# Sixty units become thirty-three in the first layer of a graph kernel, and all eight blocks take single rows

## The reference

```
dst   = sort(int(12500 * u**2))                 # 200000 edges, u uniform in 0..1
msgs  = layernorm(x)[src] * edge_weight
x1    = x + segment_sum(msgs, dst) @ W.T + b
```

```
h      = layernorm(x1) @ W_gat                  # 16 values a node: 4 heads x 4 experts
e      = leaky_relu(a_src[src] + a_dst[dst])
alpha  = segment_softmax(e, dst)
scores = layernorm(segment_sum(h[src] * alpha, dst) + b_gat), mean over heads
top 2 of the 4 scores are the gates
out    = x1 + sum_e gate_e * (gelu(y @ W1[e] + b1[e]) @ W2[e] + b2[e])   # y = layernorm(x1)
```

## Time and profile before

| | us |
|---|---|
| median of 3 runs | 3705.21 (3705.07 to 3710.14) |
| the profiled execution | 3709.83 |
| its span in the profile | 3708.0 |
| PE busy | 3033.7 (82%) |
| POOL busy | 2700.9 (73%) |
| DVE busy | 2035.0 (55%) |
| ACT busy | 819.2 (22%) |

### The profile page before, as it was taken

The page is one execution under the profiler, slowest core; times in us unless marked ns, Lnnn a source line. Parts: engine busy times, 40 slices in busy tenths (PEclk is TensorE's granted clock), DMA queues, the critical chain, the costliest instruction groups (busy, mean ns, idle before and its releaser), DMA issues. The chain is left out here.

```text
span 3708.0 us, 65908 instructions
## 1 busy us (share of the span) xinstructions
PE 3033.7 (82%) x13893; PEld 2476.2 (67%) x13894; DVE 2035.0 (55%) x6854; ACT 819.2 (22%) x2321; POOL 2700.9 (73%) x2803
## 2 busy tenths in 40 slices
PE   1666667667777777887899799999999999999748
PEld 1454445555565555665677588888888888888637
DVE  8875566576667767666664322353434343343567
ACT  6300000100111111111122222222332223222247
POOL 6677777777777777777677477777777777777573
PEclk6788887887888878788899899999999999999979
DMA  9633333434444444444344122232322222223279
GB/s 346 209 115 105 108 108 110 115 113 114 117 118 114 118 118 120 118 124 118 106 125 133 51 72 54 53 112 63 75 57 73 54 72 60 73 54 75 65 281 381
DMA packets 280932, 426.20 MB, mean 115 GB/s; under 512 B 63672, under 2 KB 214499, under 8 KB 279651
## 3 DMA queue, kind: packets, MB, share of 16 engines
q0 software_dynamic: 113760, 216.95, 23.2%
q1 hardware_dynamic: 68911, 114.88, 8.5%
q10 hardware_dynamic: 98004, 91.50, 7.6%
HBM read 317.12 MB, written 105.98 MB: 114 GB/s over the span
## 5 line engine op out<-in xcount | busy, mean ns | idle before, releaser
L712 POOL DMA_INDIRECT rows<-feats,src_t x1500 | 1459.6, 973 | 484.0 <-issue 453.5
L881 PE MATMUL node_sums<-rows,ys_ahead 128*128 x3904 | 1063.5, 432 | 479.7 <-DVE ys_ahead L942 244.8
L881 PEld LDWEIGHTS node_sums<-rows,ys_ahead 128*128 128x128 f32 x3904 | 817.0, 216 | 683.9 <-issue 550.2
L1286 POOL DMA_INDIRECT got<-row_dram,src_sorted x1010 | 977.2, 968 | 308.1 <-issue 308.1
L1369 PE MATMUL d_hidden<-d_yt,w 128*128 128x256 f32 x3136 | 711.2, 380 | 0.8 <-DVE d_yt L1455 0.8
L1380 PE MATMUL d_expert<-w,hid 128*128 128x256 f32 x3136 | 708.7, 379 | 0.0
L1380 PEld LDWEIGHTS d_expert<-w,hid 128*128 128x128 f32 x3136 | 595.8, 190 | 81.0
L1369 PEld LDWEIGHTS d_hidden<-d_yt,w 128*128 128x128 f32 x3136 | 593.7, 191 | 80.3 <-DVE d_yt L1455 1.2
L1432 DVE TENSOR_TENSOR yo<-d_expert,x_and_b 128x512 f32<-128x512 f32 x196 | 135.5, 691 | 839.8 <-PE d_expert L1380 832.2
L942 DVE TENSOR_SCALAR ys_ahead<-iota,rel,ew_t 128x128 f32<-128x128 f32 x1952 | 557.2, 361 | 66.4 <-DVE rel L938 3.8
L1313 ACT ACTIVATE hid<-d_hidden,b1c 128x256 f32<-128x256 f32 x784 | 324.4, 471 | 982.5 <-PE d_hidden L1369 793.4
(11 more groups left out here) (303 smaller groups left out, 2315.0 us busy)
## 6 DMA issues: line engine op xcount, KB each, us to landing
y_dram<-yo ACTq DMA_DIRECT2D x196, 256.0 KB
ys<-y_dram SPq DMA_DIRECT2D x36, 1024.0 KB, 9.2
got<-row_dram SPq DMA_DIRECT2D x1792, 0.1 KB
rows<-feats,src_t POOLq DMA_INDIRECT x1500
got<-row_dram,src_sorted POOLq DMA_INDIRECT x1010, 2.4
ys_ahead<-y_dram SPq DMA_DIRECT2D x13, 1024.0 KB, 9.1
x_dram<-edge_plan ACTq DMA_DIRECT2D x98, 128.0 KB
d_x<-x_dram ACTq DMA_DIRECT2D x49, 256.0 KB
```

The costliest lines, as they stand in the source:

```text
L712: pool.indirect_dma_start(rows[:, g % RING, j, :], None, feats, bass.IndirectOffsetOnAxis(ap=m.src_t[:, g * GT + j:g * GT + j + 1], axis=0 ...
L881: t = pe.matmul(psA[:, ds(((code >> 1) & 1) * 512, FEAT)], hot[:, r, j, :], rows[:, ds((code >> 2) & (RING - 1), 1), j, :], start=False, s ...
L1286: pool.indirect_dma_start(got[:, k, j, 0:ROWF], None, m.row_dram, bass.IndirectOffsetOnAxis(ap=m.src_sorted[:, BEGIN[b] + j:BEGIN[b] + j + ...
```

## The change

The loop is cut into 33 units. Behind each of the first 16, DVE makes four histogram pieces and then one whole sort piece; units 16 to 23 have a sort piece only (unit 16 also the positions), units 24 to 32 have nothing. PE counts the four pieces in the same unit, and makes the transposes at the end of the unit whose sort piece asks for them. In the second stage the last block takes single rows too, and those of block 0 are issued ahead of the wait for the spreads and the load of `adst`. POOL gathers 1008 columns instead of 1010.

```diff
-        PIECES, UNITS = 24, 60
...
+        PIECES, UNITS = 24, 33
+        COUNTED = 16
+        PER = HPIECES // COUNTED
```

PE, behind each unit:

```diff
-                if n >= 1:
-                    for q in hist_at[n - 1]:
-                        count(q)
+                if n < COUNTED:
+                    for q in range(PER):
+                        count(n * PER + q)
                 if n == COUNTED:
                     pe.matmul(psC[:, 0:TILES], zero_b[:, 0:P], zero_b[:, 0:TILES], start=False, stop=True
                               ).then_inc(s_hm, 1)
-                if n == COUNTED + 2:
                     pe.wait_ge(s_cnt, 1)
...
-                if n in TURN_AT:
-                    k = TURN_AT[n]
-                    pe.wait_ge(s_turn, k + 1)
+                if n >= 9 and n < PIECES - 1:
+                    pe.wait_ge(s_turn, n - 8)
                     for q in range(GCOLS // P):
...
-                if n == SORTED + 1:
+                if n == PIECES - 1:
```

DVE, behind each unit:

```diff
-                if n in sort_at:
-                    buf = sort_piece(*sort_at[n], buf)
-                if n == SORTED:
+                if n < COUNTED:
+                    for q in range(PER):
+                        hots(n * PER + q)
+                if n == COUNTED:
+                    positions()
+                if n < PIECES:
+                    buf = sort_piece(n, buf)
+                if n == PIECES - 1:
                     sort_end(buf)
-                if n == SORTED + 2:
-                    segments()
-                for q in hist_at[n]:
-                    hots(q)
-                if n == COUNTED + 1:
-                    counts()
-                if n == COUNTED + 3:
-                    positions()
```

`counts` is now the head of `positions`, and `segments` the tail of `sort_end`. The second stage:

```diff
-        single = lambda b: SINGLE if b < BLOCKS - 1 else 0
-        in_quarter = lambda b, q: max(0, min(size(b) - single(b), (q + 1) * QUARTER) - q * QUARTER)
+        in_quarter = lambda b, q: max(0, min(size(b) - SINGLE, (q + 1) * QUARTER) - q * QUARTER)
...
             ask(0)
+            single_rows(0)
             sp.wait_ge(m.s_sc, 16 * TILES)
             sp.dma_start(adst[:], m.adst_first[0:GEDGES, :].rearrange("(p j) h -> p j h", p=P)).then_inc(s_ad, 16)
-            single_rows(0)
             for b in range(BLOCKS):
-                if b + 1 < BLOCKS - 1:
+                if b + 1 < BLOCKS:
                     ask(b + 1)
                     single_rows(b + 1)
...
-                for j in range(size(b) - single(b)):
+                for j in range(size(b) - SINGLE):
...
-                if single(b):
-                    v.wait_ge(s_single, 16 * (1 + SINGLE * P) * (b + 1))
+                v.wait_ge(s_single, 16 * (1 + SINGLE * P) * (b + 1))
```

More of the change, by code:

```diff
@@ L915, in _ @@
                               ).then_inc(s_hm, 1)
-                if n in TURN_AT:
-                    k = TURN_AT[n]
-                    pe.wait_ge(s_turn, k + 1)
+                if n >= 9 and n < PIECES - 1:
+                    pe.wait_ge(s_turn, n - 8)
                     for q in range(GCOLS // P):
-                        t = pe.transpose(psT[:, q * P:(q + 1) * P], key[turned_keys[k]][:, q * P:(q + 1) * P],
+                        t = pe.transpose(psT[:, q * P:(q + 1) * P], key[turned_keys[n - 9]][:, q * P:(q + 1) * P],
                                          m.ident[:])
                     t.then_inc(s_turned, 1)
-                if n == SORTED + 1:
+                if n == PIECES - 1:
                     pe.wait_ge(s_turn, PIECES - 9)
@@ L989, in exchange, with columns @@
                 return to
-            def columns(buf, n, a, z):
-                for bit in range(bits_of(n) - 1 - a, bits_of(n) - 1 - z, -1):
+            def columns(buf, bits):
+                for bit in range(bits - 1, -1, -1):
                     buf = exchange(buf, bit)
@@ L1001, in take, with sort_piece @@
                 return buf
[L1003 to L1007, removed]
+            def sort_piece(n, buf):
+                if n < 10:
                     flip(buf, n + 1, 0)
[L1009 to L1012, removed]
+                    buf = columns(buf, n + 1)
+                else:
+                    k, back = 11 + (n - 10) // 2, (n - 10) % 2
+                    if back:
+                        buf = columns(take(1 - buf, n - 9), 10)
+                    else:
+                        buf = take(1 if buf != 1 else 0, n - 9)
+                        flip(buf, k, 10)
+                        buf = columns(buf, k - 10)
+                if 9 <= n < PIECES - 1:
                     v.sem_inc(s_turn, 1)
@@ L1037, in sort_end @@
                 c.done(v.tensor_reduce(m.link[:, 1:2], m.seg_keep[:], AX_X, ALU.min))
-            def segments():
                 v.wait_ge(s_turned, PIECES - 9)
@@ L1062, in hots, with positions @@
                 v.sem_inc(s_hh, 1)
-            def counts():
+            def positions():
                 v.wait_ge(s_hm, HPIECES + 1)
@@ L1068, in counts @@
                 v.sem_inc(s_cnt, 1)
-            def positions():
                 v.wait_ge(s_hm, HPIECES + 2)
```

## The result

The changed kernel takes 3644.98 us (3643.43 to 3646.45, 4 runs), the kernel before 3706.56 in the same comparison. The ratio is 0.9832 (0.9815 to 0.9849): 61.6 us faster, where 46 were forecast (3659, range 3638 to 3690). The profiled execution took 3643.7, its span is 3641.8.

A forecast was written before the change was run, and what follows sets the result against it. POOL was taken to bound the first layer to about 1600, PE after that. 17.5 (POOL's waits) + 30 (lag at the end) = 47.5, against it 2 for a lower clock: net -46, 3705.2 to 3659 us, range 3638 to 3690.

The forecast's parts named there:

- POOL keeps 17.5 us: First layer from 1600 on: POOL no longer waits for PE behind a full buffer of gathered groups, 17.5 us won.
- rival (d): First layer: POOL's gathers go faster as DVE's work is bunched, 40 us won, 3619; chance 0.08.
- The lag at the end: End of first layer: PE finishes 10 us behind POOL's last gather instead of 40.3, bounds 6 and 16; 30 us won.
- The colder last stages: End of first layer: PE reaches the four last `stages` with a lower clock than before, 2 us lost.
- The second stage: Its edits (SP's row order, two POOL columns fewer) cost or win 0, bounds -3 to +10; 1386 us as before.
- The units' account: First layer by groups of units, POOL's time against PE's: PE falls 28 behind in units 6 to 15, at most 58.
- the ring: POOL's 16 groups of gathered rows ahead of PE: 82 us, less 4 for a landing; when full, POOL waits.
- B: First layer: fewer interruptions of PE, so fewer cold restarts (steps at the lower clock); 60 units before, 33 after.
- A: First layer: the place of DVE's histogram and sort bursts, none in the last quarter of the units.
- (a): Units 6 to 15: slow return of the clock, or histogram pieces waiting for counts; at x = 5, 3689; chance 0.15.
- (b): Units 6 to 15: clock stays lower for the whole unit after each long idle; 104 net lost, 3809; chance 0.06.
- the signs: Trace marks expected, among them PE waiting in 16 long stretches of 25 to 30 us before 1200, last gather about 2029.

The follow-up runs named there:

- a_per8: The changed kernel with eight histogram pieces a unit in the first 8 units instead of four in 16: 3757.56 us, ratio 1.0142.
- a_no_exchange: The changed kernel without the sort's 306 two-input minima and maxima, so the keys stay unsorted: 3632.78 us, ratio 0.9803.
- b_rows: The kernel before with only the change's edits of the second stage: 3703.57 us against 3708.52, ratio 0.9991.
- a_layer: The changed kernel with the second stage of the kernel before, so only the new first layer: 3645.62 us, ratio 0.9838.
- b_count: The kernel before, 60 units and bursts in place, but PE counts a histogram piece in its own unit, not one later: 3657.87 us, ratio 0.9865.
- a_between: The changed kernel with histogram pieces between the first exchanges of the sort piece in the first 16 units, not ahead of it: 3646.35 us, ratio 0.9846.

## Why the prediction was right, and where it was short

*The bound.* Right. POOL sets the pace, PE held it up from 1600 on, and the second stage passes the gain on whole. a_per8 and a_no_exchange show the bound from both sides.

*POOL keeps 17.5 us.* It kept 17.7: between first and last gather it was idle 474.4 us before (1934.0 less 1459.6) and 456.7 after (1904.5 less 1447.8). But its last gather came 30.7 earlier: 11.8 more are shorter gathers, and 1.2 an earlier first gather. The 11.8 were put at 0 in the step "They lie beside POOL's gathers, which set the pace; I take 0", which rests on the same instructions running in both kernels; the instructions are the same, their stretches are not. It is rival (d) to three tenths of its size.

*The lag at the end*, 10 for 40.3: it is 5.9, at the lower bound of 6. Worth 34.4, not 30.

*The colder last stages*, -2: measured -1.8, at a granted clock of 0.60 from PE's last row multiplication to SP's first issue of the second stage, where it was 0.69.

*The second stage*, 0: b_rows and a_layer differ from their bases by less than can be told. `adst` was loaded 139.0 us after the first `ask`, as said, and pair 7 did not wait.

*The units' account.* The bursts were as long as worked out (37 us with ten exchanges, below). PE waited for rows 12 us before 300, 23 from 300 to 500, 13 to 700, then 0.9 in all up to 1300, 9 up to 1700 and 41 from there on: it fell behind where the account had it, in units 6 to 15, but further. The account left 20 us of the ring (78 less 58). In a_layer, which has the same first layer, POOL did wait for PE once, at the end of that stretch (its timeline):

```profile
1168.72 1.02 POOL L692 DMA_INDIRECT rows<-feats,src_t  x1 [3.29 <-PE node_sums L861]
```

So the ring filled there. In the changed kernel's own trace POOL has no wait over the usual gap, but little can be left: the change sits at the edge of what the ring covers, and a_per8 shows the price of going on.

*The cause.* Here the prediction was wrong, and that its range held was in part luck. "A unit of 60 carries a cold restart each, and late in the layer it meets a time when PE has most to do", and "that is where the ring filled", names B and A. It had the waits of 140.2 us in its rows, and used them only as a danger for the new kernel (a). They were the brake of the old one: b_count removes them alone and wins 50.7 us. The sum came near because its terms ask only that PE keeps up, whatever held it, and because the change happened to count in the same unit too. The row multiplications of b_count are as cold as before (1069.0 us busy, mean 429 ns; before 1063.5 and 432, after the change 983.9 and 406): PE had the time for cold steps.

*Rivals (a) and (b)* did not come. But the idle stretches of 25 to 30 us that they turn on, and that stand among the signs, did not come either: PE counts each piece as soon as DVE has made it, so its idle is cut into waits of up to 5.0 us for the pieces and one of some 13 for the sort, 14.2 at most. After those PE needs no longer to reach the higher clock; what 30 us would do, no run shows. POOL's last gather was over at 2015.9, not 2029, for the reason above. The timeline after the change, over a burst of four pieces and ten exchanges, from DVE's first cast at 989.4 to its last maximum at 1026.6, 37 us:

```profile
989.37 0.24 DVE L1034 CAST hist_columns<-ys_ahead 128x16 f32<-128x16 bf16 x2
...
1025.93 0.69 DVE L966 TENSOR_TENSOR seg_keep<-src_sorted 128x512 f32<-128x512 f32 x1
1026.73 1.97 PE L898 MATMUL turned<-ident,seg_keep 128*128 128x128 f32 x8 [13.15 <-DVEq L995]
...
1029.93 9.68 PE L861 MATMUL node_sums<-rows,ys_ahead 128*128 x32 [1.23 <-DVE ys_ahead L920]
```

The granted clock is 0.50 from 1005 to 1035, and 1.00 from there. Four steps take 9.68 us, where three take 5.45 at the full clock: 2.4 us over, two cold steps' worth, the same as after an idle of 4.59 or 8.18. So the rule of the Trainium skill that was weighed (TensorE: Matmul & The Clock Gate, HAM oscillation) agrees with the trace in its direction: the idle is followed by steps at the lower clock, and fewer idles leave the row multiplications less cold. The time of the kernel does not hang on it, because PE does not bound the layer.

## What to carry to other kernels

A wait of one engine for another that is small in the table can be the one that makes both work in turn: ask of each producer's buffer in which unit the consumer frees it, and free it in the same unit. Bursts beside a bounding gather queue are free as long as the ring covers the burst and what the consumer is already behind; work out both, and keep a margin, since the account here was some 20 us too hopeful. Where the same instructions run in both kernels, still look at the mean time of the bounding engine's own.

## What the runs showed of the hardware

Two-input instructions of DVE stretch POOL's indirect DMAs. I compared each gather of the first layer with DVE's instructions in the same trace. Gathers beside none of the sort's minima and maxima take 0.96 us on average in every kernel; those beside an idle DVE take 0.95, those beside the one-input instructions that build the one-hots and the histogram 0.96. Beside one or more minima and maxima they take 1.07 in the kernel before (182 gathers, 21 us over the others in sum, on 38 stretches of sort), 1.02 after the change (173 gathers, 11 us, 24 stretches) and 1.03 in a_between (216 gathers, 14 us, some 70 stretches). Without them (a_no_exchange) all 1500 take 0.96. Most of the difference between before and after is in long gathers: 18 of 1.2 to 2.2 us before, 7 of at most 1.4 after, each the first or second that meets its stretch (in a_between 16, of at most 1.5). The rest of a stretch costs 0.07 us a gather in all kernels, however long it is. The Trainium skill (GPSIMD Engine Reference, Key points) says that GpSimd shares its SBUF interfaces with VectorE and contends with instructions that have two SBUF inputs; the runs agree, and add its size here. Why some stretches hold a long gather and others none stays open.
